# Lead in another order: first gram ahead of a projection, x1 between turn and weight, two weight pieces moved on

## The reference

```python
x = _layernorm(x + _L0_attn_ref(x, ...))   # gated delta rule in chunks of 32 tokens, 4 heads
x = _layernorm(x + _L0_ffn_ref(x, ...))    # 8 experts, top 2, gelu
x = _layernorm(x + _L1_attn_ref(x, ...))   # linear recurrence over time
x = _layernorm(x + _L1_ffn_ref(x, ...))    # 128 -> 512 -> 512 -> 512 -> 128
```

```python
def body(i, a):
    row = a[..., i, :]
    upd = jnp.einsum('bhnj,bhnjk->bhnk', row, a)
    return a.at[..., i, :].add(upd)
attn = jax.lax.fori_loop(1, c, body, attn)
```

## Time and profile before

| | |
|---|---|
| median of 3 runs | 868.87 us (862.10 to 869.66) |
| profiled execution | 861.58 us |
| its span, first to last instruction | 859.7 us |
| mean granted TensorE clock | 0.969 |
| busy: TensorE, VectorE, ScalarE, GpSimd | 93%, 72%, 57%, 56% |

### The profile page before, as it was taken

The page is one execution under the profiler, slowest core; times in us unless marked ns, Lnnn a source line. Parts: engine busy times, 40 slices in busy tenths (PEclk is TensorE's granted clock), DMA queues, the critical chain, the costliest instruction groups (busy, mean ns, idle before and its releaser), DMA issues.

```text
span 859.7 us, 11901 instructions
## 1 busy us (share of the span) xinstructions
PE 795.8 (93%) x3812; PEld 618.3 (72%) x3812; DVE 614.7 (72%) x1162; ACT 487.4 (57%) x766; POOL 484.4 (56%) x507
## 2 busy tenths in 40 slices
PE   5998699789788999999989999999999999999997
PEld 3776586677467777777767678777877887766775
DVE  2777768897678758776867787768767866777553
ACT  3887246433943574367435744575467447767754
POOL 0039688777546738873785355435553454367343
PEclk9999699789979999999999999999999999999999
DMA  4134615400320110012000400110020000000000
GB/s 135 50 100 122 186 35 148 125 23 0 86 61 26 41 47 1 1 31 69 1 1 2 123 0 2 46 52 0 0 73 25 0 0 13 1 0 1 13 13 13
DMA packets 37903, 35.81 MB, mean 42 GB/s; under 512 B 1632, under 2 KB 30816, under 8 KB 37856
## 3 DMA queue, kind: packets, MB, share of 16 engines
q1 hardware_dynamic: 37856, 35.22, 14.6%
HBM read 21.85 MB, written 13.37 MB: 41 GB/s over the span
## 4 chain that ended last, share of the span: by engine, by line
PE 55%; POOL 14%; issue 8%; DVE 8%; ACT 2%; DMA 0%; DVEq 0%; ACTq 0%; POOLq 0%; SPq 0%
PE bank L439 55%; POOL tpm L1237 4%; POOL tmp L1234 4%; POOL fbl L1293 2%; POOL acc L1301 2%; DVE spread L1530 2%; DVE sexp L1546 1%; DVE yg L1556 1%; DVE fbh L1741 1%; POOL texp L1263 1%; DVE fbl L1739 1%; DVE fah L1798 0%; DMA pack<-pk 0%; DVE ttp L1429 0%; POOL fal L1332 0%
## 5 line engine op out<-in xcount | busy, mean ns | idle before, releaser
L1079 ACT ACTIVATE hf<-bank 128x512 f32<-128x512 f32 x64 | 38.4, 599 | 174.7 <-PE bank L439 169.1
L1293 POOL TENSOR_TENSOR fbl<-hf,fbh 128x512 fp32r<-128x512 f32 x64 | 82.0, 1282 | 70.6 <-DVE fbh L1741 70.6
L1234 POOL TENSOR_TENSOR tmp<-apm,tpm 128x31 f32<-128x31 f32 (+15 forms) x124 | 78.7, 635 | 53.3 <-DVE apm L1420 46.0
L439 PEld LDWEIGHTS bank<-pk,spread 128*128 128x128 f32 x640 | 80.6, 202 | 20.1 <-DVE spread L1530 14.1
L439 PE MATMUL bank<-pk,spread 128*128 128x64 f32 x640 | 83.3, 286 | 9.0 <-DVE spread L1530 8.0
L1324 POOL TENSOR_TENSOR fbl<-hf,fbh 128x512 fp32r<-128x512 f32 x28 | 36.9, 1319 | 89.0 <-DVE fbh L1798 89.0
L1237 POOL TENSOR_TENSOR tpm<-tpm,tmp 128x31 f32<-128x31 f32 (+15 forms) x124 | 78.5, 633 | 9.7
L1301 POOL TENSOR_TENSOR acc<-acc,yg 128x512 f32<-128x512 f32 x48 | 64.6, 1346 | 34.0 <-DVE yg L1556 34.0
L1739 DVE TENSOR_TENSOR fbl<-hf,fbh 128x512 fp32r<-128x512 f32 x64 | 59.6, 931 | 30.5 <-ACT fbh L1085 29.3
L1556 DVE TENSOR_TENSOR yg<-bank,gb 128x512 f32<-128x512 f32 x64 | 43.9, 685 | 35.2 <-PE bank L439 35.1
L439 PE MATMUL bank<-fal,wfh 128*128 128x512 f32 x160 | 67.6, 423 | 0.0
(11 more groups left out here) (240 smaller groups left out, 2220.3 us busy)
## 6 DMA issues: line engine op xcount, KB each, us to landing
pk<-pack SPq DMA_DIRECT2D x7, 1280.0 KB, 7.1
pack<-pk SPq DMA_DIRECT2D x5, 1280.0 KB, 6.8
ws<-in_wf SPq DMA_DIRECT2D x11, 256.0 KB, 3.0
pack<-pk SPq DMA_DIRECT2D x4, 640.0 KB, 4.1
xs<-in_xh SPq DMA_DIRECT2D x8, 262.0 KB, 4.2
xt<-in_xh SPq DMA_DIRECT2D x8, 262.0 KB, 2.9
ws<-in_wm SPq DMA_DIRECT2D x8, 256.0 KB, 2.7
tt<-ttp SPq DMA_DIRECT2D x4, 512.0 KB, 3.1
```

The costliest lines, as they stand in the source:

```text
L439: return P.matmul(out, lhsT, rhs, start=start, stop=stop, skip_group_check=skip)
L1079: A.activation(hf[:, 0, :], bank[4][:, :], ACT.Gelu).then_inc(S["gelu_done"], 1)
L1234: G.tensor_tensor(m, a, r, ALU.mult).then_inc(S["t_mul"], 1)
L1293: G.tensor_tensor(fbl[:, sl, :], hf[:, 1, :], f32(fbh[:, sh, :]), ALU.subtract)\
```

## The change

On TensorE, in tile 1 of the lead the third projection of tile 2 goes behind the two grams; projection 0 of tile 5 goes ahead of the grams of tile 4, and in ramp 1 the projections and squares move up by one place each. On VectorE the solution of tiles 0 and 1 is started ahead of the split of pieces 2 and 3, pieces 9 and 10 are split behind the turn of the first solution, 11 and 12 in ramp 1, 15 and 16 in dense stage 0, 17 and 18 in ramp 3. The weight of solution 1 is taken out of `solve_out` and put into dense stage 0. SP's queue gets the loads and stores in the order that fits, and pieces 16 and 17 change buffers, so that 17 can be loaded ahead of 16. No instruction of work is added or dropped.

```diff
-PIECE_BUF = tuple(p % 2 for p in range(NPIECE))
+PIECE_BUF = tuple(p % 2 for p in range(NPIECE - 3)) + (1, 0, 0)
...
@@ sync, ramp2 / ramp3 / dense
+                load_piece(PIECES[s][2])
+                store_pack(s)
                 store_tt(1)
-                for p in PIECES[s][2:] + PIECES[s + 1][:1]:
-                    load_piece(p)
-                store_pack(s)
                 load_piece(PIECES[s + 1][1])
+                load_piece(PIECES[s + 1][0])
...
                 load_next(a + 1)
+                load_piece(PIECES[s][2])
                 store_pack(s)
...
-                if isinstance(m, int) and m == 0:
-                    load_piece(PIECES[NT - 1][2])
@@ tensor, lead
                     beta(t + 1)
-                    for m in range(3):
-                        project(t + 1, m)
+                    project(t + 1, 0)
+                    project(t + 1, 1)
+                    if t != 1:
+                        project(t + 1, 2)
+                else:
+                    project(t + 1, 0)
                 gram(t, 0)
                 gram(t, 1)
+                if t == 1:
+                    project(t + 1, 2)
@@ tensor, ramp1
-                project(s, 0)
+                project(s, 1)
                 beta(s)
                 delta_wu(a, 0)
-                project(s, 1)
+                project(s, 2)
...
-                project(s, 2)
+                squares(s)
...
-                squares(s)
+                project(s + 1, 0)
...
                 gram(s, 1)
-                project(s + 1, 0)
                 beta(s + 1)
@@ vector
+                if p != 1:
+                    solve_weight(p)
...
-                split_pieces(PIECES[t][:2])
+                if t != 1 and t != LEAD - 1:
+                    split_pieces(PIECES[t][:2])
                 gram_rows(t, 0)
                 gram_rows(t, 1)
-                if t < LEAD - 2 or t == LEAD - 1:
-                    split_pieces(PIECES[t][2:])
                 if t == 1:
                     solve_in(0)
+                    split_pieces(PIECES[t][:2])
+                if t < LEAD - 2:
+                    split_pieces(PIECES[t][2:])
             solve_out(0)
+            split_pieces(PIECES[LEAD - 1][:2])
@@ vector, ramp1
-                split_pieces(PIECES[s])
+                split_pieces(PIECES[s - 1][2:])
...
                 delta_spread(a, 3)
+                split_pieces(PIECES[s])
                 value_rows(s)
@@ vector, ramp2
                 top_two(a)
+                gate_weights(a)
                 value_rows(s)
                 gram_rows(s, 0)
-                gate_weights(a)
@@ vector, ramp3
                 lru_gx(m)
+                split_pieces(PIECES[s][1:2])
...
                 beta_rows(s)
+                split_pieces(PIECES[s][2:])
                 gram_rows(s, 0)
@@ vector, dense
-                    if isinstance(m, int) and m == 0 and e in (1, 2, 4, 6):
-                        p = (1, 2, 4, 6).index(e)
-                        split_pieces((PIECES[NT - 2][2:] + PIECES[NT - 1])[p:p + 1])
+                    if isinstance(m, int) and m == 0 and e == 1:
+                        solve_weight(1)
+                    if isinstance(m, int) and m == 0 and e in (2, 5):
+                        split_pieces((PIECES[NT - 2][2], PIECES[NT - 1][0])[e // 4:e // 4 + 1])
```

More of the change, by code:

```diff
@@ L1430, in solve_out, with solve_weight @@
                 dve.wait_ge(S["t_turned"], p + 1)
+                if p != 1:
+                    solve_weight(p)
+            def solve_weight(p):
+                ttp = ttps[p // 3]
                 tt(ttp[:, :, :], ttp[:, :, :],
```

## The result

| | before | after |
|---|---|---|
| median | 866.2 us (861.8 to 869.7, 18 runs) | 870.9 us (867.5 to 873.1, 18 runs) |
| profiled execution | 861.58 us | 872.49 us |
| span, mean granted clock | 859.7 us, 0.969 | 870.6 us, 0.953 |

The ratio is 1.0054, with an interval of 1.0036 to 1.0072: the change makes the kernel 0.5%, or 4.7 us, slower. I had forecast 865.0, which was 3.6 us faster.

The account below looks back on a forecast made before the run. TensorE is busy 93% of the span; two GpSimd solutions in series set x1. Terms: -5.3 us up to x1, +0.7 dense 0, +1.0 piece 18, sum -3.6, from 868.9 to 865 us; 8-in-10 range 857 to 872.

Parts of the forecast that it names:

- the knock-on: Lead, VectorE tiles 2 to 4: the two centred splits delay a store and x of tile 4, some 0.5 us.
- the lead gives nothing: Rival, lead: splits cost GpSimd +2.5 us, late stores push x of tile 4, turn stays near 100; 868.7 us, 13%.
- The splits beside GpSimd: Lead: VectorE splits running beside the first solution lengthen it by net +0.8 us, bounds 0 and +2.5.
- third rival: Same as "the lead gives nothing": six VectorE instructions cost GpSimd their whole length, +2.5 us, and stores come late; 13%.
- two signs of being wrong: Up to x1: prediction is wrong if x1 doesn't wait for GpSimd, or if the clock falls in ramp 1 as well.
- The wait in the last chunk of ramp 1: Ramp 1, TensorE: piece 12's split delays the state product, giving a wait of 1 to 1.7 us.
- x1 ahead of the weight: Between the second solution's turn and x1: taking the weight out brings x1 of tile 0 forward, -1.9 us.
- Pieces 16 and 18: Dense 0 at e = 5 and ramp 3: the moved splits cost +0.7 and +1.0 us, bounds 0 and +1.6 each.
- The lead's 3.8: Lead: the first solution's turn, and with it chunk 0, moves 3.8 us earlier, bounds -5 and -1.5.
- the clock is kept: Rival, dense 0: the 2.45 us wait shrinks and half clock behind it goes; -7.9 us, 861 us, 15%.
- Half clock behind longer waits: Rival, dense 0 and 1: splits 16 and 18 lengthen waits, adding two half-clock stretches of 3.25 us; +2.9 us, 872, 14%.
- the 7.3 us between the profiled execution and the median of three: Whole kernel: the median of three runs lies 7.3 us above the profiled execution; assumed to carry over to the forecast.

Follow-up runs that it names:

- e1: Changed kernel with the store of tile 1 and x load for tile 4 ahead of the loads of pieces 4 and 5 in SyncE's queue: 866.4 us.
- e4: Changed kernel with pieces 15 to 18 split, buffered and loaded as before the change: 867.2 us, ratio 1.0017.
- e11: Changed kernel with 20 extra products nobody reads, in TensorE's waits of ramp 2 and dense 0: 867.2 us, ratio 1.0029.
- e5: Changed kernel with the edits of e1 and e4 together: 864.6 us, ratio 0.9974.
- e6: e5 with the second solution's weight back ahead of x1 and SyncE's ramp 2 order as before: 861.2 us, ratio 0.9953.
- e3: Kernel before with only the second solution's weight moved from ahead of x1 to dense stage 0, and its store after it: 867.2 us, ratio 1.0009.
- e12: e5 with extra products nobody reads, 11 in the waits of ramp 2 and 9 in that of dense 0: 858.6 us, ratio 0.9917.
- e9: e6 with extra products nobody reads, 13 in the waits of ramp 2 and 9 in that of dense 0: 857.4 us, ratio 0.9903.

## Why the prediction was wrong, point by point

**The price of SyncE's queue: the step that failed.** I wrote of the centred splits "plus some 0.5 for the knock-on", and that TensorE needs tile 4 only 8 us later. I had seen the wait of 3.22 us, and put the chain behind it at 13% as a rival ("the lead gives nothing"). The queue issues in order: in the chain above a load that waits for a split holds a store, and the store holds x. x of tile 4 was issued 5.2 us later (0.9 of it a late start), VectorE's gram rows of tile 4 ended at 100.35 in place of my 96.6, and the turn moved by 0.4 us and not by 3.8. e1 shows it: with the order of the queue changed and nothing else, turn and chunk 0 are within 0.3 us of the forecast, and the median is 4.5 us lower. So the size of the gain was right; wrong was the step that only 0.5 us stood in its way. What I should have done is follow the queue entry by entry, as I did for tile 6.

**The splits beside GpSimd.** +0.8 us forecast; the first solution took 43.85 us (53.34 to 97.19) against 43.67. The two centred splits that came under it and the two others that left it cost 0.2 us together. The +2.5 of my third rival was six times the 0.4 us of one pair of rows, and not the whole length that the rival speaks of: the six large instructions last 4.2 us in the changed kernel. The rule of the Trainium skill (SBUF — State Buffer, "Who interferes with whom") that each side blocks the other for the whole instruction would allow up to that; no run here shows it. The rival's other half, stores that start 3 us later and push x and the unit rows of tile 4 behind, so that the turn starts near 100, is what happened (100.27). I gave the whole 13%, with an argument against its first half alone, the measured 0.4 us.

**Ramp 1 and 2.** I named two signs of being wrong, that GpSimd isn't what x1 waits for and that the clock falls in ramp 1. Both came in the changed kernel's profile: the clock was 0.87 in place of 0.95 from chunk 0 to x1, and the turn began 1.9 us after GpSimd had ended (151.54 and 153.45). In e4 and e11, whose order is the same up to x1 (but for e11's fill), the clock was 0.97 and 0.98 there, and VectorE waited 3.15 and 4.76 us for GpSimd instead. So what is on the path there differs between executions, and goes with the clock. The wait in the last chunk of ramp 1 was 1.33 us, as forecast (1 to 1.7). One term was too small: from chunk 0 to the end of the second solution it was 46.5 to 47.0 us (the changed kernel, e1, e4, e5, e6) against 45.45, so 1.1 to 1.6 us where I had 0.4. In e1 it is 48.9 us from chunk 0 to x1, against 49.4 before, where I had 47.9.

**x1 ahead of the weight.** 1.9 us forecast at x1, 1.9 measured from the turn to x1 (e3). That this reaches the end is the second step that failed: neither e3 against before, nor e5 against e6, nor e12 against e9 is faster. None of the three pairs alone excludes a small gain; all three point the other way. VectorE has the same work to do either way, and in e3's profile the clock behind x1 was lower; which of the two takes the gain was not shown.

**Pieces 16 and 18.** 0.7 and 1.0 us forecast, 1.0 and 1.0 in the profiles, 3.6 us in the medians (e4). The mechanism was right and the size of the term was not: some 1.6 us remain, for which the half clock behind the wait (e11) and the unedited stretch are candidates, neither shown.

**The sum.** -3.6 forecast and +4.7 measured are 8.3 us apart. The lead's 3.8, the weight's 1.9 and the pieces' 3.6 - 1.7 = 1.9 make 7.6 of it. These single effects don't simply add: e1 and e4 gain 4.5 and 3.6 us by the medians, together in e5 6.2.

**The rivals.** The 2.45 us wait stays, as forecast (2.46 us), with half clock behind it, so the rival "the clock is kept" fell. "Half clock behind longer waits" held in e11 at 1.54 us, at 3.2 us where I had 3.25, and not in the changed kernel's profile at 1.34 us. Its premise that the length of the wait decides is too simple: in dense 1 the state product's wait of 1.03 us had half clock behind it in every profile, the one of before too (252.01, clock 0.69 in the 4 us behind it), and the wait of 2.70 us above had it in one profile and not in the other. The result is on the slower side, to which I gave 14%, but mostly for another reason.

**From the profile to the median.** I took the 7.3 us between the profiled execution and the median of three as something that moves along. The larger sample puts before at 866.2 and not at 868.9. My sum of -3.6 would have given 862.6 from there; the measured difference is +4.7. That 870.9 lies inside my 857 to 872 is luck of this kind and of a wide range: the sign was wrong.

**Left open.** What decides how long the half clock lasts behind x1, and whether it comes at all in the unedited stretch; whether e5 really lies above e6, and if so by the weight or by SyncE's order; how often the changed kernel meets half clock at e = 5.

## What to carry to other kernels

A queue that works in order is an engine on the path: when a step is moved, write down every load and store that waits for it, and everything that stands behind those in the same queue, before any gain is counted. A gain at one milestone is worth what the next engine lets through; with VectorE work that was only moved behind the milestone no gain was seen here. The waits of 1.5 and 2.4 us of TensorE in dense 0 cost twice, once themselves and once in clock, and products that nobody reads took the second part away behind the longer one. And where two profiles differ in a stretch that nobody edited, look at the granted clock there before an edit is blamed or praised.

## What the runs showed of the hardware

Nine extra products of 128x512 in a wait of 2.44 us made the stretch behind it 3.0 us shorter (11.21 us in e9, 14.21 in e6): the granted clock stayed at 1.00, where it was 0.58 in the 7.9 us behind the wait in e6 (a clock of 0.50 is 1.2 GHz, one of 1.00 is 2.4 GHz). In dense 0 waits of 1.34 us and less were not followed by half clock, one of 1.54 us was. Elsewhere the length of a wait doesn't tell: one of 1.03 us in dense 1 was followed by it in every profile, and one of 2.70 us behind dense 1 in the profile of the changed kernel (0.50 in 6 us) and not in that of before (1.00). The stretch behind x1, with several waits next to each other and products of 8 and 64 columns between them, has half clock in every profile, filled or not, for some 7 to 20 us (an estimate, summed from the granted clock of stretches of 2 us). The Trainium skill (TensorE: Matmul & The Clock Gate, "A second HAM failure mode: psum-queue depth-cycling") tells of a TensorE whose frequent small gaps between groups of products move the clock back and forth; the stretch behind x1 looks like this, though no run here isolates it.
